# Sixteen of the 208 expert groups moved into the last attention turn of an adaLN transformer block with 160 routed experts

## The reference

```python
h = _layernorm(x) * (1 + ca) + sa
x = x + ga * attention(h)                      # 16 heads, RoPE, causal softmax
h = _layernorm(x) * (1 + cb) + sb
probs = sigmoid(h @ router_w.T + expert_bias)
top_w, top_idx = top_k(probs, 8)               # normed, times 2.5, put into combine (T, 160)
h1 = silu(einsum('th,eih->eti', h, w_gate))    # 160 experts, 64 wide
routed = einsum('eti,ehi->th', h1 * combine.T[:, :, None], w_down)
shared = silu(h @ w_gate_shared.T) @ w_down_shared.T
x = x + gb * (routed + shared)
```

## Time and profile before

| what | value |
|---|---|
| median of 3 runs | 2289.61 us (2282.12 to 2296.89) |
| profiled execution, its own time | 2277.64 us |
| its span, first to last instruction | 2275.8 us |
| mean granted TensorE clock | 0.749 of full speed |

### The profile page before, as it was taken

One profiled execution on the slowest core, in us unless ns is written; L12 is line 12 of the kernel. 1 busy time (PEld: TensorE's weight loads), 2 busy tenths in 40 slices (PEclk: granted clock), 3 DMA queues, 4 the chain that ended last, 5 costly groups with the idle time before them and its releaser, 6 DMA issues.

```text
span 2275.8 us, 35239 instructions
## 1 busy us (share of the span) xinstructions
PE 1500.7 (66%) x11142; PEld 789.0 (35%) x11142; DVE 1191.4 (52%) x4183; ACT 823.8 (36%) x1761; POOL 1142.4 (50%) x1190
## 2 busy tenths in 40 slices
PE   5668787787878778777876659333456656666630
PEld 2223333333333333333333436222244444444520
DVE  4768768777677767777753426152232221222262
ACT  1244444444444444444442213112233333333410
POOL 2001555556545555555554450455666666666355
PEclk9988778778777777777777779666666676667765
DMA  6585555455554555555335569456588878776751
GB/s 222 149 250 164 177 169 170 143 175 161 168 162 131 160 170 166 144 175 150 104 88 175 179 210 317 153 156 188 164 272 248 252 232 244 228 233 221 245 167 61
DMA packets 296966, 417.81 MB, mean 184 GB/s; under 512 B 46523, under 2 KB 155342, under 8 KB 296654
## 3 DMA queue, kind: packets, MB, share of 16 engines
q1 hardware_dynamic: 234062, 293.86, 43.5%
q0 software_dynamic: 32768, 67.17, 9.9%
q10 hardware_dynamic: 29952, 54.54, 6.5%
HBM read 234.24 MB, written 181.16 MB: 183 GB/s over the span
## 4 chain that ended last, share of the span: by engine, by line
PE 37%; another core or an unknown queue 21%; DVE 20%; issue 10%; ACT 4%; DMA 3%; POOL 2%; ACTq 1%; SPq 1%; POOLq 0%; DVEq 0%
DVE shelf L575 9%; PE bank L715 6%; PE bank L1478 5%; PE bank L1458 5%; PE bank L1436 4%; PE bank L565 3%; PE bank L652 2%; PE bank L459 2%; PE bank L892 2%; DVE xn L863 1%; POOL vh L1529 1%; PE bank L448 1%; DMA pages<-h,pos_s 1%; ACT v_ext L1492 1%
## 5 line engine op out<-in xcount | busy, mean ns | idle before, releaser
L1529 POOL DMA_INDIRECT vh<-results,pos_all x512 | 500.2, 977 | 413.5 <-PE bank L1478 139.1
L789 POOL DMA_INDIRECT pages<-h,pos_s x512 | 500.5, 978 | 345.5 <-PE bank L565 126.4
L575 DVE CUSTOM_DVE_ANT_0 shelf<-bank,cb_all 128x512 bf16<-128x512 f32 (+3 forms) x1024 | 443.9, 483 | 171.6 <-PE bank L565 95.1
L679 ACT ACTIVATE prob<-bank 128x512 f32<-128x512 f32 x640 | 348.1, 595 | 396.7 <-PE bank L664 300.8
L1478 PE MATMUL bank<-prob,ke 64*128 64x128 f32 x1664 | 201.6, 377 | 318.8 <-issue 172.2
L1542 DVE TENSOR_REDUCE oT<-vh 128x128 f32<-128x1024 f32 x64 | 121.0, 1891 | 391.5 <-DMA out<-oT 209.8
L565 PE MATMUL bank<-km,qm 64*128 64x512 bf16 (+3 forms) x1024 | 213.0, 356 | 136.7 <-DVE rmax L575 96.3
L1478 PEld LDWEIGHTS bank<-prob,ke 64*128 64x128 f32 x1664 | 152.1, 253 | 382.2 <-issue 215.5
L1458 PE MATMUL bank<-qe,prob 128*64 128x128 f32 x1664 | 185.6, 361 | 90.4 <-issue 47.3
L715 PE MATMUL bank<-prob,v_ext 128*32 128x512 f32 (+3 forms) x2048 | 240.7, 551 | 1.0 <-ACT prob L679 0.6
L1492 ACT ACTIVATE v_ext<-bank 128x256 f32<-128x256 f32 x360 | 121.8, 382 | 283.6 <-remote 165.2
(11 more groups left out here) (180 smaller groups left out, 1779.0 us busy)
## 6 DMA issues: line engine op xcount, KB each, us to landing
pages<-free_rows SPq DMA_DIRECT2D x52, 1024.0 KB
prob<-pages SPq DMA_DIRECT2D x208, 256.0 KB
results<-v_ext ACTq DMA_DIRECT2D x208, 256.0 KB
prob<-wexp SPq DMA_DIRECT2D x512, 96.0 KB
prob<-wpack SPq DMA_DIRECT2D x80, 256.0 KB
qm<-q_stacks SPq DMA_DIRECT2D x64, 256.0 KB
km<-k_stacks SPq DMA_DIRECT2D x64, 256.0 KB
qe<-q_stacks SPq DMA_DIRECT2D x64, 256.0 KB
```

What stands on the lines that cost most here:

```text
L575: last = e.tensor_tensor_reduce(out=masked[:, g % 2, c0:c0 + (i + 1) * P], in0=MX[g % 2][:, c0:c0 + (i + 1) * P], in1=mask_w[:, S - (i + 1 ...
L679: e.activation(prob[:, slot, :], ST[g % 3][:, :], ACT.Exp, scale=SCALE).then_inc(s_exa, 1)
L789: e.indirect_dma_start(out=pages, in_=h2[:, t, :], in_offset=None, out_offset=bass.IndirectOffsetOnAxis(ap=pos_s[:, t * TOPK + k:t * TOPK ...
L1529: e.indirect_dma_start(out=y8[:, i, k, :], out_offset=None, in_=results[0:ready * 4 * GRP * P, :], in_offset=bass.IndirectOffsetOnAxis(ap= ...
```

## The change

`LATE` goes from 14 to 12: the first page set holds twelve sequences and has 136 groups, the second four and 72; all scatters to the first set are issued before the last turn. A new stream `soon()` runs groups 0 to 15 in pairs in turn 15, in banks 0 and 1 alone, each pair with its own two-deep buffers for rows (`qm`, `km`) and weights (`shelf`). The `gate_step`s and `table(0)` go from turn 15 to the tail. `FIRST`, `EARLY`, `SPREAD`, `SWITCH` and `PUTS` move on by 14 to 16 groups, so the tail holds groups 16 to 45. The diff, cut to its core:

```diff
-LATE = 14
+LATE = 12
-SWITCH = 56
-PUTS = 64
+SOON = 16
+SWITCH = 70
+PUTS = 80
...
-                streams.append(([gate_step(q) for q in range(4)], 0.05, 0.6))
-                streams.append((table(0), 0.55, 0.9))
+                streams.append((soon(), 0.0, 0.98, 0.6))
...
-        FIRST, EARLY, SPREAD = 30, 62, 32
+        FIRST, EARLY, SPREAD = 46, 76, 46
...
+        def soon_load(e, m):
+            if m == 0:
+                e.wait_ge(s_scat, 16 * NT * TOPK * LATE)
+                e.wait_ge(s_mxd, NB * 4 * UNITS)
...
+            wait(e, s_T, 2 * (m - 1))
+            for G in (2 * m, 2 * m + 1):
+                e.dma_start(soon_x[m % 2][:, G % 2, :], b_rows(pages, G)).then_inc(s_xl[G % DEEP], 16)
+            wait(e, s_Y, 2 * (m - 1))
+            for G in (2 * m, 2 * m + 1):
+                e.dma_start(soon_w[m % 2][:, G % 2, :], wpack[G * P:(G + 1) * P, :]).then_inc(s_wl[G % DEEP], 16)
+        def soon_step(m):
+            groups = (2 * m, 2 * m + 1)
+            def tr(e):
...
+                wait(e, s_YD, 2 * m)
+                wait(e, s_YA, 2 * m)
+                for G in groups:
+                    e.wait_ge(s_xl[G % DEEP], 16 * (G // DEEP + 1))
+                    for q in range(GRP):
+                        last = e.transpose(TX[G % 2][:, :].rearrange("d (p q) -> d q p", q=GRP)[:, q, :],
+                                           soon_x[m % 2][:, G % 2, q * D:(q + 1) * D], ident)
+                last.then_inc(s_T, 2)
+            def xt_even(e):
+                e.wait_ge(s_T, 2 * m + 2)
+                if m == 0:
+                    pre_a.wait(e, "k_2", NB - 1)
+                    pre_g.wait(e, "k_3", NB - 1)
+                wait(e, s_G, 2 * m)
+                e.tensor_copy(soon_T[:, 0:GRP * P], TX[0][:, :]).then_inc(s_XT, 1)
+            def xt_odd(e):
+                e.wait_ge(s_T, 2 * m + 2)
+                if m == 0:
+                    pre_g.wait(e, "k_3", NB - 1)
+                wait(e, s_G, 2 * m)
+                e.activation(soon_T[:, GRP * P:2 * GRP * P], TX[1][:, :], ACT.Identity).then_inc(s_XT, 1)
+            def gate(e):
+                e.wait_ge(s_XT, 2 * m + 2)
+                for G in groups:
+                    e.wait_ge(s_wl[G % DEEP], weights_in(G))
+                    for j in range(GRP):
+                        half = 64 * (j % 2)
+                        last = e.matmul(TX[G % 2][half:half + 64, (j // 2) * P:(j // 2 + 1) * P], w_gate(G, j),
+                                        soon_T[:, (G % 2 * GRP + j) * P:(G % 2 * GRP + j + 1) * P], start=True, stop=True)
+                last.then_inc(s_G, 2)
+            def silu(e):
+                e.wait_ge(s_G, 2 * m + 2)
+                if m == 0:
+                    pre_p.wait(e, "v", NB - 1)
+                wait(e, s_Y, 2 * m)
+                for two in range(2):
+                    e.activation(soon_h[:, two * 2 * P:(two + 1) * 2 * P], TX[two][:, 0:2 * P], ACT.Silu).then_inc(s_H, 1)
+            def down(e):
+                e.wait_ge(s_H, 2 * m + 2)
+                for j in range(2 * GRP):
+                    half = 64 * (j % 2)
+                    last = e.matmul(TX[j % 2][:, (j // 2) * D:(j // 2 + 1) * D],
+                                    soon_h[half:half + 64, (j // 2) * P:(j // 2 + 1) * P],
+                                    w_down(2 * m + j // GRP, j % GRP), start=True, stop=True)
+                last.then_inc(s_Y, 2)
+            def y_out(e, par, s_mine):
+                e.wait_ge(s_Y, 2 * m + 2)
+                for g in range(2 if m else 0):
+                    e.wait_ge(s_ys[(2 * m - 2 + g) % 4], 16 * ((2 * m - 2 + g) // 4 + 1))
+                dst, src = soon_y[:, par::2, :], TX[par][:, :].rearrange("p (j d) -> p j d", d=D)
+                if par == 0:
+                    e.tensor_copy(dst, src).then_inc(s_mine, 2)
+                else:
+                    e.activation(dst, src, ACT.Identity).then_inc(s_mine, 2)
+            def store(e):
+                e.wait_ge(s_YD, 2 * m + 2)
+                e.wait_ge(s_YA, 2 * m + 2)
+                for G in groups:
+                    e.dma_start(b_rows(results, G), work[:, 4 + G % 2, :]).then_inc(s_ys[G % 4], 16)
+            return [{"pe": tr, "dve": xt_even, "act": xt_odd}, {"pe": gate, "act": silu},
+                    {"pe": down, "dve": lambda e: y_out(e, 0, s_YD), "act": lambda e: y_out(e, 1, s_YA)}, {"act": store}]
+        def soon():
+            loads = [{"sp": lambda e, m=m: soon_load(e, m)} for m in range(SOON // 2)]
+            steps = loads[0:2]
+            for m in range(SOON // 2):
+                steps += soon_step(m) + loads[m + 2:m + 3]
+            return steps
...
             if name == "sp":
                 for h in range(2):
                     e.wait_ge(s_pv, 4 * NB - 1 + h)
-                    if h == 0:
-                        e.wait_ge(s_scat, 16 * NT * TOPK * LATE)
-                    for G in range(HALFD * h, HALFD * (h + 1)):
+                    for G in range(SOON + HALFD * h, SOON + HALFD * (h + 1)):
                         rows_in(e, G)
-                    b_load(e, h)
+                    b_load(e, SOON // 4 + h)
+                run(name, e, table(0)[-1:])
                 table_in(e, 0)
...
-            shared_at.setdefault(SPREAD + 2 + 7 * k // 4, []).append(st)
+            shared_at.setdefault(SPREAD + 1 + 7 * k // 4, []).append(st)
...
-                         (post(NB - 1), 0.25, 0.7, 0.6), (beside(scatters(NB - 2), 0), 0.24, 0.62),
-                         (beside(scatters(NB - 1), 15), 0.71, 1.0),
-                         ([b_step(G) for G in range(FIRST)], 0.13, 1.0, 0.0))
+                         (post(NB - 1), 0.25, 0.7, 0.6), (beside(scatters(NB - 2), SOON), 0.24, 0.62),
+                         (beside(scatters(NB - 1), SOON + 15), 0.71, 1.0),
+                         ([gate_step(q) for q in range(4)], 0.1, 0.45), (table(0)[:1], 0.0, 0.0), ([{"dve": st["dve"]} for st in table(0)[1:]], 0.1, 0.2),
+                         ([b_step(G) for G in range(SOON, FIRST)], 0.13, 1.0, 0.0))
```

More of the change, by code:

```diff
@@ L1140, in dg @@
                     pre_p.wait(e, "v", NB - 1)
+                    e.wait_ge(s_Y, SOON)
                     e.memset(ones_sq, 1.0).then_inc(s_gbd, 1)
@@ L1158, in take @@
                     e.wait_ge(s_mxp, NB * 4 * UNITS)
+                    e.wait_ge(s_T, SOON)
                 e.wait_ge(s_gbp, q + 1)
@@ L1322, in count @@
                         pre_g.wait(e, "k_3", NB - 1)
+                        for g in range(4):
+                            e.wait_ge(s_ys[g], 16 * (SOON // 4))
                     else:
@@ L1375, in entry, with w_known @@
             return G * GRP - NE if G < NGRP1 else G * GRP - 2 * NE
+        soon_x = [t[:, :, :, :].rearrange("p a h t -> p (a h t)").bitcast(F32).rearrange("p (g c) -> p g c", g=2)
+                  for t in (qm, km)]
+        soon_w = [shelf[:, 4 * r:4 * r + 4, :].rearrange("p a t -> p (a t)").bitcast(F32).rearrange("p (g c) -> p g c", g=2)
+                  for r in range(2)]
+        soon_T = work[:, 2:4, :].rearrange("p g t -> p (g t)")
+        soon_h = work[:, 0, :]
+        soon_y = work[:, 4:6, :].rearrange("p g (j d) -> p (g j) d", d=D)
+        def w_known(G):
+            return soon_w[G // 2 % 2][:, G % 2, :] if G < SOON else w_flat[G % DEEP]
         def w_gate(G, j):
             return w_in[G % DEEP][:, j, 0:INTER] if entry(G) is not None else \
-                w_flat[G % DEEP][:, j * INTER:(j + 1) * INTER]
+                w_known(G)[:, j * INTER:(j + 1) * INTER]
         def w_down(G, j):
@@ L1383, in w_down @@
             at = GRP * INTER + (j // 2) * D
-            return w_in[G % DEEP][half, j, INTER:WROW] if entry(G) is not None else w_flat[G % DEEP][half, at:at + D]
+            return w_in[G % DEEP][half, j, INTER:WROW] if entry(G) is not None else w_known(G)[half, at:at + D]
         def weights_in(G):
@@ L1409, in b_load @@
                          .then_inc(s_wl[G % DEEP], 16)
-                if G >= DEEP:
+                if G >= SOON + DEEP:
                     rows_in(e, G)
@@ L1424, in y_store @@
             e.dma_start(b_rows(results, G), y_sb[:, G % 4, :, :].rearrange("p j d -> p (j d)")).then_inc(s_ys[G % 4], 16)
+        def soon_load(e, m):
+            if m == 0:
+                e.wait_ge(s_scat, 16 * NT * TOPK * LATE)
+                e.wait_ge(s_mxd, NB * 4 * UNITS)
+                e.wait_ge(s_rest, 32 * NB)
+                for w in "qk":
+                    e.wait_ge(s_store[w], 16 * 6 * NB)
+            wait(e, s_T, 2 * (m - 1))
[4 more added lines that the diff above has]
+                e.dma_start(soon_w[m % 2][:, G % 2, :], wpack[G * P:(G + 1) * P, :]).then_inc(s_wl[G % DEEP], 16)
@@ L1431, in tr @@
                 e.wait_ge(s_xl[G % DEEP], 16 * (G // DEEP + 1))
-                if G == 0:
-                    e.wait_ge(s_mxd, NB * 4 * UNITS)
+                if G < SOON + 2:
+                    e.wait_ge(s_YD, SOON)
+                    e.wait_ge(s_YA, SOON)
```

(15 more changed lines are left out.)

8 lines of the change are left out of this document (5 added, 3 removed).

## The result

The changed kernel takes 2337.17 us, median of 4 runs (2334.22 to 2346.02). The kernel before, run beside it, takes 2290.55 (2282.12 to 2296.89). The ratio is 1.0216, interval 1.0181 to 1.0252: slower, outside the predicted range and on the other side of no change.

A forecast was written before the change was run, and what follows sets the result against it. It held that nothing is full in turn 15 and that unbroken gather runs stop the groups almost wholly later. Terms -41 + 26 + 5 - 45 + 33 = -22 us, from the median 2289.6, gave 2268 us, range 2226 to 2314.

The forecast's parts named there:

- turn 15 to the last exponential: Turn 15: sixteen groups added, PE filled to 0.80 as in turn 14, 105 us in all, +26 us.
- gate steps, table; 30 tail groups: Tail: gate steps and table move there and add PE, DVE and SP work, +5 us.
- 16 groups leave: After the tail: the stretch from group 30 to 45 goes, -41 us.
- group 46 to 84: After the tail: first gathers come in smaller runs, 203 us to group 84 against 248, -45 us.
- group 84 to the end: End: sequences 12 and 13 wait for 184 and 192 stored groups and go in runs, +33 us.
- The later `EARLY` and `SWITCH` keep their distance to the shared steps: nothing: Moved schedule constants: they keep their distance to the shared expert's steps, so they cost or give nothing.
- rival 1: At the end groups go on during runs, four runs end to end: -19 instead of +33, 2216 us; chance 0.12.
- the walk from group 46: Groups 46 to 84 reckoned piece by piece: short gather runs, one run of 32, then three a group; 203 us.
- rival 4: Start of gathers: short runs cost as much as long ones, nothing saved: +23, 2313 us; chance 0.12.
- rival 2: Turn 15 hardly grows, since PE fills and its clock rises: 5 instead of 26, 2247 us; chance 0.12.
- rival 3: Turn 15: scatter runs hold the pairs' loads: +71 instead of +26, 2313 us; chance 0.12.

The follow-up runs named there:

- e2_puts80: The kernel before with `PUTS` 80 instead of 64 and nothing else: 2374.5 us, 1.0252 of the kernel before.
- e1_putpace: The changed kernel with output stores issued for tile T at group 80 + 8T/3 instead of 80 + 13T/4: 2329.2 us, 1.0081 of the kernel before.
- e3_late12: The kernel before with `LATE` 12 instead of 14 and nothing else: 2333.9 us, 1.0118 of the kernel before.
- e4_smooth: The kernel before with gather i waiting for group 51 + i/3 instead of 40 + i/3: 2258.2 us, 0.9784 of the kernel before.
- e5_after_smooth: The changed kernel with the edits of e1_putpace and e4_smooth: 2272.8 us, 0.985 of the kernel before.
- experiment 8: The kernel before, each pair of gathers waiting until the pair before has landed, allowance unchanged: 2675.1 us, 1.1598 of the kernel before.
- e7_smooth_spread: The kernel before with the edits of e4_smooth and e6_after_spread: 2250.1 us, 0.9758 of the kernel before.
- e6_after_spread: The changed kernel with sequence 13's last 14 scatters paced by the last exponential units, not sent in one run: 2344.1 us, 1.0173 of the kernel before.
- e9_no_silu: e6_after_spread with a plain copy in place of the pairs' Silu, on the third chip: 1982.9 us in one run.
- e10_after_all: The changed kernel with the edits of e1_putpace, e4_smooth and e6_after_spread, on the third chip: 1984.8 us, 0.9863 of the kernel before.
- e11_before_both: The kernel of e7_smooth_spread run on the third chip: 2005.5 us, 1.0012 of the kernel before.

## Why the prediction was wrong

| term | predicted us | measured us |
|---|---|---|
| ahead of turn 15 | 0 | +5.5 (1134.0 to 1139.5) |
| turn 15 to the last exponential | +26 | +26.3 (88.4 to 114.7) |
| gate steps, table; 30 tail groups | +5 | +6.2 (134.1 to 140.3) |
| 16 groups leave | -41 | -40.8 |
| group 46 to 84 | -45 | -6.0 |
| group 84 to the end | +33 | +65.3 (625.4 to 690.7) |
| sum | -22 | +56.5 |

**The end failed, by 32 us.** The step that failed is the one that isn't there: "The later `EARLY` and `SWITCH` keep their distance to the shared steps: nothing" passes over `PUTS`. It is a wait that the change adds on SP's queue, and behind it stand DVE's sums and then POOL. e2_puts80 shows it alone (61 us), and in the change e1_putpace takes 22 us of it away from group 84 on. That sequences 12 and 13 wait for 184 and 192 stored groups was right, and its price about so: 33 was put, e3_late12 has 27 by the ratio (12 to 42) and 38 by the traces, and e1_putpace has 269.4 us from group 169 on against 234.3, 35 more. The starts are 61, 46 and 59 us apart in the change and 59, 58 and 50 in e3_late12, all over the 41 of rival 1, which is out on these chips. The other 10 us or so of the 32 stay open; 8 of them lie between group 84 and 169 (399.2 us in e1_putpace against 391.1), where the prediction put nothing.

**The start failed, by 39 us.** The step is the walk from group 46, which let short runs of gathers be cheaper than long ones. It let 120 gathers go by group 84 (24, five times 8, 32 and three for each of the last eight groups) in 203 us, 0.9 us a gather over the 95 us of the groups. In the change 129 went in 242.4 us, 1.1 us each, nearly the 1.2 of the long runs before (estimates as in experiment 4). The loss came in two parts. Group 72 came at 134.4 us and not at 119, after four runs of 8: 15 us. The other 24 were lost behind it. There sequence 2 and over half of sequence 3, 50 gathers, went out as one run, for the allowance, counted from group 40, had grown to more than a hundred gathers by then: group 78 at 169.3, group 79 at 219.7. I had put one run of 32 there and stopped asking at the place where I thought the allowance was reached. So rival 4, short runs as dear as long ones, was right for this term, with a chance of 0.12.

What does make gathers cheaper is three for each group from the start: e4_smooth takes 170 us for the stretch in before and e5_after_smooth 173 in the change, in part because fewer gathers fall into it. That an unbroken run all but stops the engines was right; that it stops them by taking the place of other transfers isn't shown (experiment 8). The prediction read the idle DMA engines from 1440 to 1445 as speaking against round-robin between queues. The row can't decide that, as SP took 13.30 us for four issues there and left the engines little to go round to.

**Turn 15 came out at +26.3 against +26, and that is in part luck.** It was put at 105 us up to the tail's first unit with PE busy 0.8 of it, and took 96.1 with 0.74, 17.7 more than before; the last units then took 18.6 instead of 10.0, since the scatter run moved onto them, and this made up the rest. Without that run the pairs still cost 27.7 us (e7_smooth_spread 74.7, e6_after_spread 102.4), and on the third chip 24.5 to 26.0. So it isn't the stall, and rival 2, a turn that hardly grows, is out. So is rival 3, loads held by scatters: no wait for rows or weights is among the larger ones of the turn. PE's work was less than reckoned (71.3 us, not 84), and of ACT's table loads, which I had put beside other work, at least a part lies on the path (e9_no_silu). Nothing shows that PE's fill set the size.

**What doesn't add up.** 5.5 us lie ahead of turn 15, where the change only moves the clearing of pages. Sequence 14's first exponential starts at 1087.5 us in before and at 1093.2 in the change, but at 1098.2 to 1104.7 in the eight runs that followed, whether the first page set was long or short: the profiled execution of before was an early one. By the medians the change costs 47 us.

## What to carry to other kernels

When a change shifts a schedule, list every constant by which one engine's queue paces another (here loads, outputs, sums, gathers) and work out for each pair from which step on the one overtakes the other; a transfer that looks idle at the end of a chain can hold its head 16 steps later. On the chips of the first kind a backlog let out at once cost more than the same work let out evenly (50 us here), on the third chip it didn't; and a sum that walks through a backlog must ask at each step how large it is. Work moved under another stage isn't free when both hand over in strict order on the same engines: 41 us of groups cost 26 us in the turn and 6 in the tail here.

## What the runs showed of the hardware

**Runs of gathers all but stop the other engines on some chips and not on others.** On the first chips a run leaves the groups nothing: PE 0.00 of 5 us and DMA 0.27 busy, and SP's own issuing slows from 1.94 to 13.30 us for four loads. So it is the engines' steps that are held up, and the transfers go missing at least in part because they aren't issued. On the third chip, POOL issues at the same rate (3.78 us busy in 5, as in the earlier trace rows), SP issues four loads in 1.94 us, and PE and the DMA engines go on at full load:

```profile
core 0: us, PE busy (x) PEld busy (x) DVE busy (x) ACT busy (x) POOL busy (x), PEclk, DMA share, GB/s
1330.00:1335.00 5.00, 4.60 (x56) 3.19 (x52) 3.36 (x8) 2.11 (x5) 3.78 (x5) 1.00 0.99 317
1304.00:1425.30 121.30, 93.51 (x924) 63.81 (x921) 76.15 (x126) 46.08 (x112) 90.69 (x96) 0.93 1.03 339
...
1860.00:1980.00 120.00, 0.00 (x0) 0.00 (x0) 44.18 (x49) 0.00 (x0) 88.03 (x93) 0.50 0.22 58
```

These rows are of e10_after_all. Its 16 runs of gathers follow one another at 40 to 43 us from 1320.3 to the end, and the last three lie behind the last group: there POOL's issuing of 512 gathers sets the end, as my rival 1 had it, and before takes 12 to 13% less time than on the other chips. The Trainium skill ("DMA: Bandwidth & Descriptors", section "Queues, rings and completion order") says that each DMA engine goes round the queues that have work; the third chip's rows agree with it; those of the others can't test it, since there the loads were issued late. e7_smooth_spread and e11_before_both are one kernel, one traced on each kind: 165.5 and 134.5 us for groups 46 to 84, 2245.9 and 1989.7 in all, with the same 417.81 MB moved. Why the chips differ, and what holds the engines' steps up in a run, is open; nothing in the traces tells. Everything above on the change's 1.0216 holds for the first kind, and the change as it stands wasn't run on the third chip.

**ACT and PE stop in such runs too,** with "remote" or "issue" as what they wait for: 9.3 us of ACT at 1246.9, 4.6 at 1235.6, and PE's products of the last units 1.4 us apart. Spreading the scatters took 12.3 us off that stretch in the change (114.7 to 102.4) and 13.7 in before (88.4 to 74.7; 15 against e4_smooth's 90.0), without changing the number of scatters.
